# Where the causal pattern of a mixture attention is added: VectorE in the banks, or products on TensorE

## What is computed

```python
q, k = apply_rotary(q, k, position_ids, l)
scores = jnp.einsum('bhqd,bhkd->bhqk', q * scale, k)
mask = jnp.tril(jnp.ones((q.shape[-2], k.shape[-2]), dtype=bool))
scores = jnp.where(mask, scores, jnp.finfo(jnp.float32).min)
p = jax.nn.softmax(scores)
ctx = jnp.einsum('bhqk,bhkd->bhqd', p, v)
```

## Time and profile before

| | us |
|---|---|
| median of 3 runs | 1388.88 |
| their range | 1388.78 to 1389.87 |
| the profiled execution's own time | 1388.42 |
| its span, first to last instruction | 1386.5 |
| TensorE busy (matmuls) | 1314.9 |
| TensorE weight loads | 1055.5 |
| VectorE busy | 764.6 |
| ScalarE busy | 473.6 |
| GpSimd busy | 451.3 |

### The profile page before, as it was taken

One profiled execution on the slowest core, in us unless ns is written; L12 is line 12 of the kernel. 1 busy time (PEld: TensorE's weight loads), 2 busy tenths in 40 slices (PEclk: granted clock), 3 DMA queues, 4 the chain that ended last, 5 costly groups with the idle time before them and its releaser, 6 DMA issues.

```text
span 1386.5 us, 26030 instructions
## 1 busy us (share of the span) xinstructions
PE 1314.9 (95%) x10995; PEld 1055.5 (76%) x10995; DVE 764.6 (55%) x1361; ACT 473.6 (34%) x785; POOL 451.3 (33%) x558
## 2 busy tenths in 40 slices
PE   7977899999999999999999999989899999999988
PEld 5755677787886777888888888876678787787766
DVE  4455575666666656353344434445667566666553
ACT  3323333423324223244345443433332333313321
POOL 1143444444344332211111111324334344334332
PEclk9978999999999999999999999999999999999999
DMA  9010000000001001200000000011000000000000
GB/s 324 7 61 1 2 2 2 1 2 1 2 6 42 2 20 39 86 17 1 1 0 1 0 1 0 1 41 42 2 2 2 1 17 1 2 16 2 1 17 17
DMA packets 19903, 27.31 MB, mean 20 GB/s; under 512 B 3433, under 2 KB 15553, under 8 KB 19521
## 3 DMA queue, kind: packets, MB, share of 16 engines
q1 hardware_dynamic: 19008, 24.20, 5.2%
q10 hardware_dynamic: 768, 1.26, 0.3%
HBM read 23.35 MB, written 2.10 MB: 18 GB/s over the span
## 4 chain that ended last, share of the span: by engine, by line
PE 84%; DVE 6%; ACT 4%; POOL 3%; issue 2%; DMA 0%; SPq 0%; ACTq 0%; DVEq 0%; POOLq 0%
PE bank L1418 6%; PE bank L1708 6%; PE bank L1673 5%; PE bank L1678 5%; PE bank L1562 5%; PE bank L1914 4%; PE bank L1878 4%; PE bank L1921 4%; PE row_banks L1512 4%; PE row_banks L1822 3%; PE row_banks L1545 3%; PE bank L1480 3%; PE bank L1697 3%; PE bank L1411 3%; PE row_banks L1517 2%; ACT room L2032 2%
## 5 line engine op out<-in xcount | busy, mean ns | idle before, releaser
L1269 POOL TENSOR_SCALAR_AFFINE_SELECT room<-room 128x1024 f32<-128x1024 f32 x64 | 70.7, 1108 | 186.4 <-ACT room L2032 186.4
L2274 DVE TENSOR_REDUCE room<-row_banks 128x4 f32<-128x512 f32 (+1 forms) x128 | 116.4, 952 | 23.4 <-PE row_banks L1517 23.0
L2032 ACT ACTIVATE room<-row_banks 128x1536 f32<-128x1536 f32 x64 | 92.9, 1451 | 89.6 <-PE row_banks L1545 89.6
L1708 PE MATMUL bank<-room,down_w 128*128 128x256 f32 x384 | 94.4, 386 | 0.5 <-DVE room L2374 0.5
L2288 DVE RECIPROCAL room<-bank 128x256 f32<-128x256 f32 x32 | 56.1, 1754 | 59.3 <-PE bank L1562 59.3
L2064 ACT ACTIVATE room<-bank 128x256 f32<-128x256 f32 x96 | 36.4, 383 | 147.7 <-PE bank L1678 136.7
L1231 POOL TENSOR_TENSOR room<-room 128x256 f32<-128x256 f32 x32 | 24.5, 766 | 171.8 <-ACT room L2044 171.8
L1708 PEld LDWEIGHTS bank<-room,down_w 128*128 128x128 f32 x384 | 69.6, 190 | 13.6 <-issue 4.9
L1342 POOL TENSOR_TENSOR room<-room 128x512 f32<-128x512 f32 x32 | 33.7, 1070 | 133.1 <-DVE room L2474 132.9
L1545 PE MATMUL row_banks<-room 32*128 32x256 f32 (+1 forms) x1024 | 62.1, 357 | 9.7 <-ACT room L2032 4.6
L1545 PEld LDWEIGHTS row_banks<-room 32*128 32x128 f32 x1024 | 48.9, 191 | 27.6 <-issue 15.6
(11 more groups left out here) (242 smaller groups left out, 3037.8 us busy)
## 6 DMA issues: line engine op xcount, KB each, us to landing
out_x<-wq SPq DMA_DIRECT2D x8, 256.0 KB, 2.3
qkv<-in_L_xattn_v_qkv SPq DMA_DIRECT2D x2, 768.0 KB, 6.4
qkv<-in_L_xattn_l_qkv SPq DMA_DIRECT2D x2, 768.0 KB, 9.2
gate_w<-in_L_xattn_v_gate SPq DMA_DIRECT2D x2, 640.0 KB, 8.4
gate_w<-in_L_xattn_l_gate SPq DMA_DIRECT2D x2, 640.0 KB, 7.6
up_w<-in_L_xattn_v_up SPq DMA_DIRECT2D x2, 640.0 KB, 6.2
up_w<-in_L_xattn_l_up SPq DMA_DIRECT2D x2, 640.0 KB, 6.5
down_w<-in_L_xattn_v_down SPq DMA_DIRECT2D x2, 640.0 KB, 6.4
```

The lines of the kernel that those rows point to most:

```text
L1269: pool.affine_select(out=diagonal, in_=diagonal, compare_op=ALU.is_ge, fill=0.0, base=0, pattern=[[0, 8], [1, P]], channel_multiplier=-1)\
L1708: return pe.matmul(ff_bank[0][:, t * S:(t + 1) * S], down_w[:, f, t * P:(t + 1) * P], hid[:, i, :], start=(i == t == 0), stop=(i == UPS - ...
L2032: act.activation(probs[w % 2], row_banks[:, :, 0:3 * P], ACT.Exp).then_inc(*ATT_ACT.does(e, f"exp{w}"))
L2274: last = dve.tensor_reduce(dst, row_banks[:, :, P * i:P + S * i], X, ALU.max, negate=True)
```

## The change

The four products of L1517 and their gap in the order of work go. `first_scores` ends with its 16 matmul instructions. `maximum` begins with one VectorE addition over the eight diagonal blocks of the four banks, in place, and its two reductions wait for it. The pattern stays f32; its bf16 copy on GpSimd and the bf16 identity go. All starts and due times are new, so the order of stages is new on each engine: of 1150 TensorE stages 874 keep their order relative to each other, of 723 on VectorE 541, of 613 on ScalarE 461, of 401 on GpSimd 291. The order on SyncE is the same.

```diff
-    "first_scores": ("att", "pe", "s1#"), "maximum": ("att", "dve", "max#"), "turn_max": ("att", "pe", "nm"),
+    "first_scores": ("att", "pe", "s1#"), "maximum": ("att", "dve", "mask# max#"), "turn_max": ("att", "pe", "nm"),
...
-        ident_bf = sb("ident_bf", [P, P], BF16)
         causal_f = sb("causal_f", [P, P])
-        causal = sb("causal", [P, P], BF16)
...
-                pool.wait_ge(pro_pool, 2)
-                pool.tensor_copy(causal[:], causal_f[:]).then_inc(pro_pool, 1)
...
                         if e == 0:
                             pe.wait_ge(*F_DVE.did(B - 1, "y"))
-                            pe.wait_ge(pro_pool, 3)
+                            pe.wait_ge(pro_pool, 2)
...
-                            pe.matmul(row_banks[:, j, P * i:P + S * i], q_one[e % 2][par][r, t, i * P:(i + 1) * P],
-                                      k_one[e % 2][par][r, t, 0:P * (i + 1)], start=(i == 0), stop=False,
+                            last = pe.matmul(row_banks[:, j, P * i:P + S * i], q_one[e % 2][par][r, t, i * P:(i + 1) * P],
+                                      k_one[e % 2][par][r, t, 0:P * (i + 1)], start=(i == 0), stop=(i == 1),
                                       skip_group_check=True)
-                    for j in range(4):
-                        diagonal = row_banks[:, j, 0:3 * P].rearrange("p (b n) -> p b n", n=P)[:, 0:3:2, :]
-                        last = pe.matmul(diagonal, ident_bf[:], causal[:].unsqueeze(1).to_broadcast([P, 2, P]),
-                                         start=False, stop=True, skip_group_check=True)
                     last.then_inc(*ATT_PE.does(e, f"s1{w}"))
...
-                dve.wait_ge(const_in, 16)
-                dve.tensor_copy(ident_bf[:], ident)
...
                     dve.wait_ge(*ATT_PE.did(e, f"s1{w}"))
                     if e == w == 0:
                         dve.wait_ge(mot_zeroed, 1)
+                        dve.wait_ge(pro_pool, 2)
+                    diagonal = row_banks.rearrange("p j (b n) -> p (j b) n", n=P)[:, 0:16:2, :]
+                    dve.tensor_tensor(diagonal, diagonal, causal_f[:].unsqueeze(1).to_broadcast([P, 8, P]), ALU.add)\
+                       .then_inc(*ATT_DVE.does(e, f"mask{w}"))
+                    dve.wait_ge(*ATT_DVE.did(e, f"mask{w}"))
                     for i in range(TT):
```

More of the change, by code:

```diff
@@ new lines, in attend_stages @@
+        put(-2046.4844, "select", 0)
+        put(-2046.4528, "select", 1)
+        put(-2031.6492, "select", 2)
+        put(-2023.6698, "select", 3)
+        put(-2005.9924, "split")
+        put(-1256.4554, "maximum", 0)
+        put(-1247.9792, "maximum", 1)
+        put(-1244.6882, "maximum", 2)
+        put(-1239.1713, "maximum", 3)
+        put(-1234.8824, "shift_q")
+        put(-1227.3552, "context", 0)
+        put(-1205.6833, "context", 1)
+        put(-839.5155, "exp", 0)
+        put(-839.3659, "exp", 1)
@@ new lines, in attend_stages @@
+        put(-832.3310, "exp", 2)
+        put(-825.4975, "exp", 3)
+        put(682.8806, "first_scores", 0)
+        put(692.8788, "first_scores", 1)
+        put(696.9633, "first_scores", 2)
+        put(706.4781, "first_scores", 3)
+        put(711.4452, "turn_max")
+        put(711.5738, "second_scores", 0)
+        put(712.2462, "second_scores", 1)
+        put(712.5332, "values", 0)
+        put(712.6310, "second_scores", 2)
+        put(712.7311, "values", 1)
+        put(712.9836, "second_scores", 3)
@@ new lines, in cross_stages @@
+        put(-988.5584, "crs_mean", 1)
+        put(-981.1853, "post_y")
+        put(-633.8915, "cross_k_out")
+        put(-628.9640, "crs_square", 0)
+        put(-626.9791, "cross_q_out")
+        put(-609.4079, "cross_exp")
+        put(-598.3070, "crs_square", 1)
+        put(899.1584, "memory")
+        put(900.8231, "dense")
+        put(913.2589, "crs_sum", 0)
+        put(917.0704, "crs_spread", 0)
+        put(922.3943, "cross_q")
+        put(923.2572, "cross_first")
+        put(927.6703, "cross_turn_max")
@@ new lines, in feed_stages @@
+        put(-1700.0183, "by_expert", 0)
+        put(-1692.8723, "late_y")
+        put(-1684.6049, "by_expert", 1)
+        put(-1680.8489, "by_expert", 2)
+        put(-1667.5493, "by_expert", 3)
+        put(-1656.7932, "by_expert", 4)
+        put(-888.8544, "hidden", 0)
+        put(-884.2268, "hidden", 1)
+        put(-875.8401, "hidden", 2)
+        put(-874.8256, "hidden", 3)
+        put(-867.4670, "hidden", 4)
+        put(-865.8312, "hidden", 5)
+        put(-825.3664, "give")
+        put(-505.8429, "tanh", 0)
@@ L895, in put @@
         at.append((time, stage, *which))
-    put(-9564.6367, "out_sent")
-    put(-24.1953, "out")
-    put(1485.6441, "turn_out")
+    put(-29.6928, "out")
+    put(1534.8106, "turn_out")
+    put(4338.0179, "out_sent")
     return at
@@ L940 @@
[L940 to L944 removed]
+    put(-15363.8070, "p_vec_out")
+    put(-15321.2287, "f_mem_out", 0)
+    put(3050.2955, "p_one_hot")
```

1204 lines of the change are left out of this document (573 added, 631 removed).

## The result

The changed kernel takes **1409.13 us** (median of 4 runs, 1407.75 to 1411.14), the one before 1389.38 beside it. The ratio is 1.0146, interval 1.0132 to 1.0161: slower by 20 us. The prediction said 1372.5, faster. Its range ended at 1390.

A forecast was written before the change was run, and what follows sets the result against it. TensorE bounds the body, round-trip latency the layers' ends. Removed products -28.8 us and added waits +12.4 us sum to -16.4, 1388.4 to 1372.0 profiled, so 1372.5 us measured; range 1359 to 1390, about 0.8.

The forecast's parts named there:

- the round trip: From first_scores through addition and maximum to the next first_scores: 4.08 us, needing 3.2 us of other TensorE work between sets.
- the short gaps of the count: Places between score sets, or before turn_max, with under 3.2 us of other TensorE work, where TensorE would wait.
- The whole order is written anew on all engines ... I count 0 and give it 3 us either way: Stages moved past each other on all engines: counted as 0, with 3 us either way in the range.
- 64 x 0.45 = 28.8 us ... In the body nothing covers this work: Removing 64 sets of pattern products and their gaps from TensorE saves 28.8 us, as TensorE has no idle there.
- the 12.4 us of short gaps: Added TensorE waits for the reductions at first_scores and turn_max, beyond those in today's time: 12.4 us.
- the 15.7 that were counted for the new order: All TensorE waits at short places in the changed order: 10.6 us between first_scores, 5.1 before turn_max.
- All of it pays: Rival: the short gaps wait for something else anyway, so the whole 28.8 us is gained, 1360.1 us; chance 0.2.
- not at its limit: Rival: TensorE's recorded busy time overlaps and the products were filling time, so no change, 1388.9 us; chance 0.1.
- the slower one: Rival: VectorE's bank writes are dear, addition 2.4 us, 1398.4 us; decided from about 2.07 us; chance 0.16.
- a layer's start that has grown by more than 5 us: Sign of a wrong forecast, at the layers' starts: the new order would be the cause; no chance given.

The follow-up runs named there:

- without a pattern: Pattern left out of the first scores, neither products nor addition: 1378.78 us in the order of before, 1390.39 in the changed kernel's order.
- with the products: The kernel before, pattern still added by bf16 products, given all starts and due times of the changed kernel: 1408.2 us, ratio 1.0143.
- the old order: Starts and due times of the kernel before; the changed kernel's code run with them, pattern added by VectorE, took 1421.61 us, ratio 1.0245.
- Kept busy: 73 small identity products put ahead of TensorE waits in layer 0 and at layer 1's start: changed kernel 1395.39 us, kernel before 1386.15.

## Why the prediction was wrong

**Right.** The kernel is bound by TensorE and by round trips at the layers' ends. The addition: 1.22 us taken, 1.229 measured, also beside GpSimd's work. VectorE at 75% in the body. The count of matmuls. And the round trip, which can be followed at the third and fourth sets of element 6, one of the short gaps of the count:

```profile
431.96 0.94 PE L1508 MATMUL row_banks<-room 32*128 32x128 f32 x16
...
432.97 1.23 DVE L2264 TENSOR_TENSOR row_banks<-row_banks,causal_f 128x1024 f32<-128x1024 f32 x1 [0.21 <-PE row_banks L1508]
...
434.24 1.82 DVE L2269 TENSOR_REDUCE room<-row_banks 128x4 f32<-128x512 f32 x2
...
434.66 0.50 PE L1423 MATMUL bank<-mean_w,room 128*128 128x1 f32 x4
...
435.97 0.15 DVE L2307 TENSOR_SCALAR room<-bank 128x2 f32<-128x2 f32 x1
...
436.11 0.94 PE L1508 MATMUL row_banks<-room 32*128 32x128 f32 x16 [0.95 <-DVE room L2269]
...
438.38 1.13 PE L1590 MATMUL bank<-room,cq_w 128*128 128x256 f32 x4 [0.96 <-DVE room L2214]
```

From start to start 4.15 us (4.08 forecast), with a wait of 0.95 (1.04 forecast).

**The step that failed most: "The whole order is written anew on all engines ... I count 0 and give it 3 us either way".** The order alone costs 11.6 us without a pattern and about 20 with the products. It had no row, and it was given the price of nothing with a narrow bound. A wider bound from rows was at hand: TensorE stands idle for some 8 to 13 us in each of three stretches at the layers' ends, and nothing said that new starts for every stage would not add as much again. What the runs show in its place are 12 us of new waits at `second_scores` and `cross_q`, and stretches at the lower clock. With them stood a term that the sum lacked altogether: the granted clock. The prediction saw the 0.94 and 0.93 of the earlier trace rows and used them only to say that products there would cost somewhat more. It asked neither what holds the clock up in the old order nor whether the new one keeps it: in layer 0 the old order has other work between the short norm products (46 to 52 us) and keeps the upper clock, and about 6 us depended on the order there.

**Second: "64 x 0.45 = 28.8 us ... In the body nothing covers this work".** The slot is 0.45 us. Its worth is 9.1 us (old order) to 17.8 (new). The busy share of 99% in the body was read as "TensorE has no idle there"; but at 22 of 64 places the products only filled a time in which the next stage's input wasn't ready, as at the spread that waits 0.54 us once they go. That accounts for 6.2 of the 19.7 us that are missing; the rest stays open. The prediction measured that slack for one waiter, `first_scores` at 0.14 us, and used it only against the addition. The same reasoning holds for the removal: what becomes free is worth no more than the slack of the next stage's own chain. Doubling the products, which needs no slack of anybody, costs 23.4 of 27.5.

**Third: the 12.4 us of short gaps.** The mechanism is as forecast: the waits at the reductions are 9.6 us of the 15.7 that were counted for the new order. The addition's whole price in the new order is 18.7. Between the profiled executions without a pattern and of the changed kernel lie 19.6 us of span: 10.9 of them are idle time of TensorE, near the waits for the reductions, and 8.7 are busy time for the same 10739 matmuls. The changed kernel is at the lower clock for 96.9 us there and the other for 73.2. So the term that is missing is the clock again. Kept busy, the two kernels have the same busy time, 1301.4 us, and their spans differ by 10.8 (the medians by 15.4). What is queued behind the longer maximum stage costs little in the new order. The wait of `cross_q` (L1590) in the timeline above may look like such a knock-on, but the same stage waits as long with the products in place of the addition:

```profile
432.75 1.13 PE L1598 MATMUL bank<-room,cq_w 128*128 128x256 f32 x4 [0.96 <-DVE room L2224]
```

It belongs to the new order and not to the addition. In the old order the knock-on is there: `cross_first` waits for the maximum, and the addition costs 42.8 us where the count gave 17.

None of the rivals was it either. "All of it pays" and "not at its limit" concern the products, and the truth lies between them; the slower one had the sign but asked for an addition of 2.07 us. A rival of the right kind, "the new order loses more at the layers' starts than the body gains", was named in the last line only ("a layer's start that has grown by more than 5 us"), without a chance. That sign was the one that came: 9.0 us by the first set of scores.

**What stays open.** Kept busy, the new order still costs 5.6 us without a pattern and 12.9 with products. In the profiled executions the lag against the old order at the last element's first set of scores is 0.6 and 8.2 us, at the end 5.4 and 12.9: so nearly 5 us lie behind that set in both pairs, in the tail of layer 3. Which stages make them, and the other 8 with products, was not found. Beyond layer 0 no experiment exchanged the order of one stretch alone, so that the four waits named above are seen in the traces and not priced each by itself. Nor is it settled how much of the clock's share is cause and how much goes along with waits.

## What to carry to other kernels

A change that rewrites the order of work is two changes; price the order by itself, with a bound from the idle time that it can double, and separate the two in the first experiment. Work freed on the bounding engine is worth at each place no more than the next stage's inputs are early by, which is to be read behind several of the freed places (here that was a part of the loss only); work added to it was paid nearly whole. Before a wait behind an edit is put down to the edit, look for it in the kernel with the same order and without the edit. Where short TensorE products stand between waits, look at the granted clock of the stretch: here 73 products of no use ahead of the waits gave back 13.7 of 1409 us.

## What the runs showed of the hardware that was not expected

- VectorE adds in place in the banks (1024 f32 for each of 128 partitions) at 1229 ns, as fast as it reduces them, 1216 ns.
- Eight f32 products of 64 columns take 1.00 us at the upper clock and 1.76 at the lower one, and a stretch stays down for 13.7 us though TensorE is 97% busy by its records in the first 10 of them (9.69 of 10.00).
- Adding 73 products made a kernel faster by 13.7 us.
- The price of the same instructions depends on the direction: 64 more sets of products cost 23.4 us, and taking the 64 sets away gave 9.1.
